# A four-layer graph network on one core: 448 edge tiles sorted on chip instead of gathered

## What is computed

```python
m_in = jnp.concatenate([h[src], h[dst], edge_attr], axis=1)
msg = jax.nn.relu(m_in @ msg_w1 + msg_b1) @ msg_w2 + msg_b2
agg = jax.ops.segment_sum(msg, dst, num_segments=h.shape[0])
upd_in = jnp.concatenate([h, agg], axis=1)
upd = jax.nn.relu(upd_in @ upd_w1 + upd_b1) @ upd_w2 + upd_b2
return h + upd
```

## Time and profile before

| | |
|---|---|
| median of 3 runs | 3737.18 us (3730.82 to 3748.77) |
| span of the profiled execution | 3756.0 us, its mean granted TensorE clock 0.949 |
| busy share | PE 89%, PE weight loads 65%, DVE 39%, ACT 34%, POOL 23% |
| edge phase in that span | about 2727 to 3739 us |

### The profile page before, as it was taken

The page is one execution under the profiler, slowest core; times in us unless marked ns, Lnnn a source line. Parts: engine busy times, 40 slices in busy tenths (PEclk is TensorE's granted clock), DMA queues, the critical chain, the costliest instruction groups (busy, mean ns, idle before and its releaser), DMA issues. The chain is left out here.

```text
span 3756.0 us, 88102 instructions
## 1 busy us (share of the span) xinstructions
PE 3351.3 (89%) x23534; PEld 2436.9 (65%) x23535; DVE 1468.0 (39%) x4294; ACT 1270.1 (34%) x4020; POOL 856.6 (23%) x928
## 2 busy tenths in 40 slices
PE   5989999999998899997899999999967887888887
PEld 3656666777754444443799999998745555555555
DVE  7877777777720400003442111113322232333333
ACT  6766777778820400003432221123311111111111
POOL 2000000000020000000000000001277777777775
PEclk8999999999999999997999999999988898889999
DMA  3012222333368297791343222224233333333332
GB/s 67 18 51 68 68 84 85 102 103 117 104 172 212 70 231 189 188 221 46 79 124 102 76 76 76 76 73 118 68 78 79 79 78 79 77 77 79 78 77 71
DMA packets 118672, 367.65 MB, mean 98 GB/s; under 512 B 32906, under 2 KB 74360, under 8 KB 105766
## 3 DMA queue, kind: packets, MB, share of 16 engines
q1 hardware_dynamic: 89572, 310.74, 30.7%
q0 software_dynamic: 25664, 51.90, 6.2%
q10 hardware_dynamic: 3154, 1.60, 0.2%
HBM read 280.52 MB, written 83.62 MB: 97 GB/s over the span
## 5 line engine op out<-in xcount | busy, mean ns | idle before, releaser
L2348 POOL DMA_INDIRECT edge_rows<-src_table,src_idx x784 | 761.9, 972 | 239.9 <-issue 238.6
L2492 ACT ACTIVATE edge_act<-edge_ps 128x512 f32<-128x512 f32 x196 | 117.1, 597 | 892.4 <-PE edge_ps L2450 892.4
L2464 PEld LDWEIGHTS edge_ps<-edge_hot,edge_act 128*128 128x128 f32 x1760 | 263.7, 224 | 157.9 <-issue 157.2
L2450 PE MATMUL edge_ps<-edge_rows,ident 128*128 128x512 f32 x392 | 267.8, 771 | 104.5 <-DMA edge_rows<-src_table,src_idx 103.7
L1190 PE MATMUL prop_ps<-rows,y 125*128 125x500 f32 (+1 forms) x798 | 307.9, 544 | 17.5 <-DMA rows<-adj_rows 10.6
L821 PE MATMUL build_ps<-build_place 128*128 128x325 bf16 (+1 forms) x1380 | 298.9, 298 | 4.9 <-ACT build_place L749 3.0
L749 ACT ACTIVATE build_place<-build_place,w 128x128 f32<-128x128 bf16 x690 | 259.9, 405 | 121.3 <-DVE build_place L704 88.5
L2464 PE MATMUL edge_ps<-edge_hot,edge_act 128*128 x1760 | 282.2, 312 | 5.5 <-issue 4.6
L2442 PE MATMUL edge_ps<-m_store,edge_hot_t 125*128 x2640 | 228.1, 230 | 55.2 <-issue 35.3
L704 DVE TENSOR_SCALAR build_place<-key_id,lane,one_w 128x128 f32<-128x128 f16 x690 | 236.4, 343 | 85.9 <-PE build_ps L821 41.5
L1190 PEld LDWEIGHTS prop_ps<-rows,y 125*128 125x128 f32 x798 | 143.7, 192 | 179.6 <-issue 152.8
(11 more groups left out here) (379 smaller groups left out, 5815.9 us busy)
## 6 DMA issues: line engine op xcount, KB each, us to landing
rows<-adj_rows SPq DMA_DIRECT2D x62, 1367.2 KB
cnt_panels<-build_cnt SPq DMA_DIRECT2D x50, 683.6 KB
adj_rows<-rows SPq DMA_DIRECT2D x25, 1367.2 KB
n<-cnt_panels SPq DMA_DIRECT2D x40, 683.6 KB
orders_panel<-cnt_panels SPq DMA_DIRECT2D x40, 683.6 KB
edge_dst_row<-dst_rows SPq DMA_DIRECT2D x196, 125.0 KB
h<-cnt_panels SPq DMA_DIRECT2D x20, 683.6 KB
edge_rows<-src_table,src_idx POOLq DMA_INDIRECT x784
```

The source lines that it names most:

```text
L2348: pool.indirect_dma_start(rows[s][:, i, :], None, dr.table, bass.IndirectOffsetOnAxis(ap=g.src_idx[:, t:t + 1], axis=0)).then_inc(s_rows[s ...
L2450: pe.matmul(ps[:, s, :], g.ident[:], rows[s][:].rearrange("p a k -> p (a k)"), start=False, stop=True, skip_group_check=True).then_inc(s_p ...
L2464: last = pe.matmul(bank, act[s][:, i, :], hot[:, bass.ds(here, 1), i * B:(i + 1) * B].rearrange("p a k -> p (a k)"), start=i == 0, stop=i ...
```

## The change

448 of the 784 tiles (the first 57,344 edges) are sorted by (destination block, source block) on chip, into tiles in which all edges have one source block and one destination block; P[src] then comes from 4 x 3 matmuls of a one-hot matrix with the three bf16 parts of P in SBUF, at a register address for each tile, and not from a gather. The other 336 tiles are gathered as before.

- Setup: 172,032 slots of 8 bytes in DRAM are filled with "empty".
- Propagation, pass 0: class `EdgeSort` computes each edge's slot on DVE (50 counting passes, then 25 rounds of mask, scan and predicated copy over 448 elements), with 25 scalings on ACT and four small PE steps after rows 4, 9, 11 and 13.
- Orders: POOL scatters 448 x 128 edges (8 bytes each) to their slots by 448 indirect DMAs. P and Q are both kept as three bf16 parts (`pq`); the buffers of the end move; the weight loads are 14 and not 10, behind the scatters and behind `s_tr`.
- Edge phase: the slots are read back; DVE, ACT and PE make the tile tables, and SP writes them to DRAM and waits. 42 mixed rounds of two sorted and two gathered groups, then `more` rounds of four sorted groups (a value computed on chip).

```diff
+SORTED = 448
+SLOTS = 4
+GROUP = 4
+ROUNDS = (E // TE + 1 - SORTED + 2 * GROUP - 1) // (2 * GROUP)
+AHEAD = 4
...
@@ class EdgeSort @@
+    def vector(self, v):
...
+        for at in range(2 * NB):
...
+            v.tensor_scalar(self.unread[at % 4], self.both, float(at), None, ALU.is_equal, ALU.add,
+                            accum_out=self.hist[:, at // NB, at % NB:at % NB + 1]).then_inc(self.s_hist, 1)
...
+        mask(0)
+        for s in range(NB):
+            if s + 1 < NB:
+                mask(s + 1)
+            count(s)
+            if s:
+                place(s - 1)
...
@@ propagation_phase, tensor @@
+                    if h == 0 and at in sort.AFTER:
+                        sort.tensor(pe, sort.AFTER[at])
...
@@ orders_phase, gpsimd @@
+            pool.dma_start(dr.w_rows, g.bias_rows[:, BIAS_EDGE:BIAS_EDGE + D]).then_inc(s_w, 16)
+            for j in range(SORTED):
+                turn, lot = divmod(j // LOT, len(s_scattered))
+                if turn and j % LOT == 0:
+                    pool.wait_ge(s_scattered[lot], turn * LOT * 16)
+                pool.indirect_dma_start(dr.slots, bass.IndirectOffsetOnAxis(ap=g.src_idx[:, j:j + 1], axis=0),
+                                        g.pay[:, j, :], None).then_inc(s_scattered[lot], 16)
+            for sem in s_scattered:
+                pool.wait_ge(sem, SORTED // len(s_scattered) * 16)
+            pool.wait_ge(s_w, 16)
+            pool.wait_ge(s_tr, TURNED)
             pool.wait_ge(s_t, (K - 1) * NB)
...
+            for p in range(3):
+                pool.dma_start(a3.pq[B:128, :, p, 0, :],
+                               dr.w_rows[p:p + 1, :].unsqueeze(1).to_broadcast([3, NB, D])).then_inc(s_w, 16)
-            pool.wait_ge(s_w, 16 * 10)
+            pool.wait_ge(s_w, 16 * 14)
...
+class SrcBlocks(Blocks):
+    BITS = 5
...
+    def each(self, s, ahead):
+        both = self.value(s, ahead, 1 << (self.BITS * GROUP))
+        for i in range(GROUP):
+            self.eng.reg_mov(self.now[i], (both >> (self.BITS * i)) & ((1 << self.BITS) - 1))
+        return [self.eng.snap(r, min_val=0, max_val=NB - 1) for r in self.now]
...
@@ edge_phase, sync @@
+            def sorted_group(n, s):
+                for to, of, sem in ((src_row[s], rows_of[1], s_src[s]), (dst_row[s], rows_of[0], s_dst[s])):
+                    sp.dma_start(to[:], of[bass.ds(n, 1), :].to_broadcast([B, W])).then_inc(sem, 16)
+                sp.dma_start(hot_s[s][B:128, :], parts_of[:, bass.ds(n, 1), :].rearrange("i a k -> i (a k)")
+                             ).then_inc(s_ea[s], 16)
...
@@ edge_phase, vector @@
+            def turned(r, s, ahead, wide):
+                if sorted_slot(s, wide):
+                    v.wait_ge(s_src[s], r * 16 + 16 if s not in GATHERED else r * 16 + (16 - 16 * ROUNDS))
+                    v.tensor_scalar(hot_s[s][0:B, :], src_row[s][:], lane[0:B, :], None, ALU.is_equal).then_inc(s_hot_s[s], 1)
...
@@ edge_phase, tensor @@
+            def sources_of(s, at, p):
+                for i in range(GT):
+                    last = pe.matmul(place(s, i), hot_s[s][:, i * 128:(i + 1) * 128],
+                                     a3.pq[:, bass.ds(at[i], 1), p, 0, :].rearrange("p a k -> p (a k)"),
+                                     start=p == 0 and i == 0, stop=p == 2, skip_group_check=True)
+                return last
+
+            def inputs(r, s, ahead, wide):
+                at = src_blocks.each(s, ahead) if sorted_slot(s, wide) else None
                 pe.wait_ge(s_act[s], r + 1)
                 pe.wait_ge(s_ea[s], r * 16 + 16)
...
+                if at is not None:
+                    pe.wait_ge(s_hot_s[s], r + 1 if s not in GATHERED else r + (1 - ROUNDS))
+                    sources_of(s, at, 0)
+                else:
...
                 blocks.each(s, ahead, one)
-                pe.wait_ge(s_rows[s], r * (16 * GT) + 16 * GT)
-                pe.matmul(ps[:, s, :], g.ident[:], rows[s][:].rearrange("p a k -> p (a k)"), start=False, stop=True,
-                          skip_group_check=True).then_inc(s_pre[s], 1)
+                if at is not None:
+                    sources_of(s, at, 1)
+                    sources_of(s, at, 2).then_inc(s_pre[s], 1)
+                else:
...
+            def advance(r):
                 blocks.advance(r)
+                src_blocks.advance(r)
...
+            with pe.Fori(0, ROUNDS) as r:
+                round_of(r, False, False)
+                advance(r)
+            with pe.Fori(ROUNDS, pe.snap(more + LAST)) as r:
+                round_of(r, True, False)
+                advance(r)
+            round_of(pe.snap(more + LAST), True, True)
```

More of the change, by code:

```diff
@@ L1118, in _ @@
         def _(pool):
+            sort.pool(pool)
             biases.pool(pool)
@@ L1671, in orders_phase @@
         s_out = ph.sem("out")
+        s_scattered = [ph.sem(f"scattered{i}") for i in range(4)]
+        LOT = 8
         block = ph.ctx.enter_context(nc.Block())
@@ L2278, in advance, with value, __init__ @@
             self.eng.reg_mov(c, n)
-        self.eng.load(self.nxt, self.g.groups[0:1, bass.ds(r * SLOTS + 2 * SLOTS, SLOTS)])
+        self.eng.load(self.nxt, self.table[0:1, bass.ds(r * SLOTS + 2 * SLOTS, SLOTS)])
+    def value(self, s, ahead, most):
+        return self.eng.snap((self.nxt if ahead else self.cur)[s], min_val=0, max_val=most)
+class DstBlocks(Blocks):
+    def __init__(self, eng, table):
+        super().__init__(eng, table, "group")
+        self.now = [eng.alloc_register(name=f"group_now{k}") for k in range(2)]
     def each(self, s, ahead, body):
-        both = self.eng.snap((self.nxt if ahead else self.cur)[s], min_val=0, max_val=NT * RANGE)
+        both = self.value(s, ahead, NT * RANGE)
         self.eng.reg_mov(self.now[0], both >> RANGE_BITS)
@@ L2310, in edge_phase @@
         s_dst = [ph.sem(f"dst{s}") for s in range(SLOTS)]
+        s_src = [ph.sem(f"src{s}") for s in range(SLOTS)]
+        s_hot_s = [ph.sem(f"hot_s{s}") for s in range(SLOTS)]
         s_ea = [ph.sem(f"ea{s}") for s in range(SLOTS)]
@@ L2319, in edge_phase @@
         s_tick = ph.sem("tick")
+        s_raw = ph.sem("raw")
+        s_lanes = ph.sem("lanes")
+        s_dst16 = ph.sem("dst16")
+        s_dstf = ph.sem("dstf")
+        s_cut = [ph.sem(f"cut{i}") for i in range(3)]
+        s_left = ph.sem("left")
+        s_sorted = ph.sem("sorted")
+        s_turned = ph.sem("turned")
+        s_dcol = ph.sem("dcol")
+        s_limits = ph.sem("limits")
+        s_row = ph.sem("row")
+        s_table = ph.sem("table")
+        s_d = ph.sem("d")
         block = ph.ctx.enter_context(nc.Block())
@@ L2355, in _ @@
+            v.memset(in_mixed(sources, 2), 0)
+            v.memset(ps[:, SUMS, 0:B], 0.0)
+            v.memset(a3.agg_t[:], 0.0).then_inc(s_added, 1)
+            tables()
+            v.wait_ge(s_table, 1)
+            blocks = DstBlocks(v, dsts)
+            more = v.value_load(g.rounds[0:1, 0:1], min_val=1, max_val=MORE)
             made = Counter(v)
@@ L2418, in _ @@
         def _(pe):
-            blocks = Blocks(pe, g)
+            pe.wait_ge(s_dstf, 1)
+            for c in range(PER_LOT):
+                last = pe.transpose(ps[:, c // 4, c % 4 * LOTS:(c % 4 + 1) * LOTS], raw[:, c, :, 0], g.ident[0:LOTS, 0:LOTS])
+                if c % 4 == 3:
+                    last.then_inc(s_turned, 1)
+            pe.wait_ge(s_limits, 1)
+            for k in range(2):
+                for n in range(3):
+                    last = pe.transpose(ps[0:1, 5 + k, 0:MOST_GROUPS].rearrange("a (q n) -> a n q", n=3)[:, n, :], both[:, k, n:n + 1], g.ident[0:LOTS, 0:LOTS])
+            last.then_inc(s_row, 1)
+            pe.wait_ge(s_table, 1)
+            pe.wait_ge(s_dcol, 3)
+            blocks = DstBlocks(pe, dsts)
+            src_blocks = SrcBlocks(pe, sources)
+            more = pe.value_load(g.rounds[0:1, 0:1], min_val=1, max_val=MORE)
             used = Counter(pe)
```

464 lines of the change are left out of this document (384 added, 80 removed).

## The result

The kernel after takes 4196.9 us (median of 4 runs, 4191.4 to 4204.1), before 3739.8 us in the same comparison: a ratio of 1.122, 95% interval 1.120 to 1.124. The profiled execution spans 4202.3 us with a mean granted clock of 0.851.

The account below looks back on a forecast made before the run. POOL's gathers bound the edge phase before, PE's sequencer after: loop +405, opening +33, sort +3, weights +6, setup and barriers +4, +451 us on 3756.0, less 18.8 for the profiled execution: 4188 us, range 3880 to 4380, chance 0.68.

Parts of the forecast that it names:

- What bounds PE: Edge phase, PE: a group that waits for no row takes 3.69 us by the sequencer, 2.90 us by the array.
- Sorted group 6.2 us: Edge phase, PE: 3.69 us plus 21 more sequencer instructions at 0.12 us; bounds 4.8 and 7.2 us; 152 such groups.
- Gathered group 3.85 us, round's end 1.8, pass 2.5: Edge phase, PE: us for each of 84 gathered groups, 59 round ends and 16 more additional passes.
- Opening +33: Edge phase, first load to first matmul: 37 us instead of 3.6, for reading slots and making tables; range 15 to 50.
- Sort +3 (0 to 25): Propagation pass 0: the sort on DVE adds 3 us, up to 25 where the scan is slower.
- Scatter hidden: Orders, POOL: 573 us of scatter from 1812.3 us ends at 2385, before the weight loads of 2526.6; adds nothing.
- The rival that it is late: Orders: at 147 ns a write the scatter lasts to 2576 us and PE waits for weights; +49 us, 4235 us; chance 0.08.
- Weights +6, setup and barriers +4: Later weight loads with two more stores at the end, +6 us; fills and more semaphores to clear, +4 us (0 to 10).
- Rival 1: Edge phase: PE's sequencer runs ahead of the array, a sorted group takes 3.4 us by DVE; total 3619 us; chance 0.09.
- Rival 2: Edge phase, PE: added register instructions are fused or overlapped, 4.3 us a sorted group; total 3900 us; chance 0.12.
- Rival 4: Whole kernel: no change of pace and other costs small, 3737 us within 0.5%; chance 0.03.
- The signs: Edge phase: PE gaps "issue", round of four 26.6 us, first matmul 37 us behind first load, POOL busy slices 20 to 26.

## Why the prediction was right

4188 us was forecast, 4196.9 measured, inside the range; by its steps:

- *What bounds PE* (3.69 us by the sequencer, 2.90 by the array): the mechanism is shown by the run without gathers, by the doubled matmuls and by the one price for each recorded instruction in these runs.
- *Sorted group 6.2 us*: 6.1 to 6.2. The 21 instructions cost 0.130 us each together, 0.11 for the unpacking, 0.10 to 0.12 for loops and branches; 0.12 was taken. The compare-and-branch price of 108 ns cited from the Trainium skill (Advanced Engine Details and Errata, Control Flow Timing) is near these. No run leaves out branches alone; in the trace of after the sequencer's next instruction starts 137 ns after a compare-and-branch (median of 561), in that of before 125, so the trace has them dearer.
- *Gathered group 3.85 us, round's end 1.8, pass 2.5*: across a round's end there are 7.94 us, 1.82 more than within a round, as forecast. A mixed round without an additional pass takes 21.8 us (forecast 21.9), which leaves 3.9 us for a gathered group. An additional pass costs some 3.2 us (an estimate, fitted over the mixed rounds): mis-sized by 11 us in all, which the sorted groups (6.12 instead of 6.2, 12 us) make up by chance. Loop forecast 1411, measured 1416.7.
- *Opening +33*: +30.9, with the read and the passes as costed.
- *Sort +3 (0 to 25)*: +5.3 in pass 0, not where the forecast put it: DVE was in time, while PE's own steps (3.0 us) and its waits for rows (4.2 more, of which no run tells the cause) had no term. 25 rounds take 1.93 us each, not 2.2, and end 19 us ahead of need. The scan takes 1.15 us, the copy over as many elements 0.64: with the half throughput that the Trainium skill gives for the built-in scan (DVE: opcode table, instruction layouts, handler registers and perf-mode slots, on feedback) the trace agrees as far as these two rows tell, but mask (0.28) and copy are cheaper than I had them, so the end near 1216 us that followed from it did not come.
- *Scatter hidden*: 1811.4 to 2381.6 us, 570 us against 573 forecast, and PE not touched. The rival that it is late is out on these chips, and both its prices were wrong by their unit: the 48 and 147 ns are for a packet, and the sum took 57,344 writes for as many packets. The trace has 14,268 packets for the scatter (1812 to 2382 us), at 2.1% of the 16 engines' time: 13 ns each. So what the Trainium skill says of packets below 512 bytes (DMA: Bandwidth & Descriptors, Specifications) has no visible price here, and the conclusion that by it the rival decides did not hold. On two other chips the scatter (and the gathers) holds up everything, in another way than small packets filling the DMA engines.
- *Weights +6, setup and barriers +4, with the sort +13*: +4.7 in the orders and +5.3 in pass 0, so nearly right by stage. The two profiled executions show only +2.4 up to the edge phase, since the passes between are 9.0 us shorter in the one of after by their own spread. The 2.6 us behind the last sum had no term.
- *18.8 us taken off for the profiled execution*: the one of after lies only 5.4 us above its median. This and the terms (451 against 446.3) account for the 8.9 us that the forecast is low; so close a hit is luck, given the spread of 9 us in stages that the change leaves alone.
- *Rival 1 and its break-even, 3.2 us a sorted group*: the run with fixed sources has 3.66 us in the rows shown and 3.5 by its rounds (15.8 us less 1.8, by four), for which the prediction's sum gives a loss of 0.3 x 152 = 46 us; 36 were measured. *Rival 2* (4.3 us) is out: none of the added register instructions ran beside others for nothing. *Rival 4* is out by the interval.
- *The signs*: a round of four took 26.3 us (26.6), the first matmul came 34.5 us behind the first load (37), the gaps are "issue". One sign was misplaced: POOL is busy in slices 18 to 23 (scatter) and 27 to 35 (gathers), not 20 to 26.

## What to carry to other kernels

Before an engine's work is made dynamic, count the register, wait and branch instructions of one turn in the lowered program, and price them by a turn in the trace that waited for nothing: here 0.10 to 0.13 us each on PE, and one address instruction for each matmul whose operand moves. Moving work off a saturated engine pays only up to the spare time of the next one (here 154 us), so size it by the two paces and not by how much can be moved, and stage by stage: two bounds that follow each other don't average (983 us instead of 952 with 64 tiles). Take the comparison on more than one chip when many small indirect DMAs are added.

## What the runs showed of the hardware

- PE's sequencer took 0.129 to 0.134 us for each recorded register, wait or branch instruction in six kernels, with 12 matmuls more or fewer gathers beside them alike.
- Twelve more matmuls in a group raised the granted clock from 0.50 to 0.86 and cost nothing. A low granted clock can be the mark of an engine that waits for its own sequencer.
- On two chips of those used, before takes 3986 and 3991 us and not 3740. While POOL scatters there, the other engines show "issue" and "remote" waits of up to 223 us with the DMA engines 2% busy. It lasts as long as the scatter: 600 us for 448 (1812.7 to 2413.2), 122 for 96 (1819 to 1940). Without a scatter the orders run undisturbed on such a chip (before with ten more increments: PE busy 100.00 of 100 us, 1900 to 2000), and the phase of the gathers alone is longer. The wide rounds, which have no indirect DMA, run at 21.1 us there as elsewhere. What is held up (fetching of instructions, semaphores) no run tells.
- Successive semaphore increments on PE stand 0.151 us apart.
